# A fused attention and feed-forward kernel: the order of work inside an attention step is changed

## The reference

```
xn = layernorm(x);  Q = xn @ Wq / sqrt(32);  K = ctx @ Wk;  V = ctx @ Wv
scores = Q K^T + slope[head] * (key_pos - query_pos)     (masked)
w = softmax(scores);  x = x + tanh(g_xattn) * (w V) @ Wo
h = silu(bit_linear(layernorm(x), w_gate)) * bit_linear(layernorm(x), w_up)
x = x + tanh(g_ffn) * bit_linear(rms_norm(h), w_down)
```

## Time and profile before

| | |
|---|---|
| median of 3 runs | 536.34 us (533.21 to 541.49) |
| profiled execution: its own time | 538.78 us |
| its span, first to last instruction | 537.0 us |
| mean granted TensorE clock | 0.978 of full |
| TensorE busy | 478.4 us, 89% of the span |
| VectorE busy | 367.5 us, 68% |
| ScalarE busy | 329.6 us, 61% |
| GpSimd busy | 234.1 us, 44% |

### The profile page before, as it was taken

The page is one execution under the profiler, slowest core; times in us unless marked ns, Lnnn a source line. Parts: engine busy times, 40 slices in busy tenths (PEclk is TensorE's granted clock), DMA queues, the critical chain, the costliest instruction groups (busy, mean ns, idle before and its releaser), DMA issues.

```text
span 537.0 us, 8363 instructions
## 1 busy us (share of the span) xinstructions
PE 478.4 (89%) x2887; PEld 301.7 (56%) x2902; DVE 367.5 (68%) x674; ACT 329.6 (61%) x560; POOL 234.1 (44%) x250
## 2 busy tenths in 40 slices
PE   2599979998989999997889999879899999999966
PEld 1599979997954444443444445435454555555522
DVE  4777634466555888885697785376777777777782
ACT  0366637565436656664756676577677777777760
POOL 1000000000146687855263670157666667677641
PEclk9999998999899999998999999999999999999988
DMA  7869897999748788879667721002533333333323
GB/s 189 266 186 406 331 354 279 236 345 289 150 88 201 176 184 203 192 153 237 147 136 172 159 96 73 29 0 39 119 79 79 78 78 78 78 74 77 75 52 68
DMA packets 55875, 83.94 MB, mean 156 GB/s; under 512 B 30787, under 2 KB 42259, under 8 KB 53919
## 3 DMA queue, kind: packets, MB, share of 16 engines
q1 hardware_dynamic: 50654, 58.30, 43.2%
q0 software_dynamic: 3456, 12.58, 8.7%
q10 hardware_dynamic: 1728, 12.58, 6.8%
HBM read 57.94 MB, written 9.85 MB: 126 GB/s over the span
## 4 chain that ended last, share of the span: by engine, by line
PE 56%; DMA 14%; DVE 11%; ACT 9%; issue 5%; POOL 2%; SPq 1%; ACTq 0%; POOLq 0%; DVEq 0%
DMA ct<-ctx_t 7%; PE bank L1335 6%; PE wide L1410 6%; PE bank L1325 6%; PE wide L1311 6%; PE bank L1420 6%; PE wide L1242 6%; PE bank L1242 6%; PE bank L1338 5%; PE bank L1283 5%; DMA yq<-y_int 3%; ACT p_t L709 3%; DVE row_max L982 3%; DMA qs<-nm_t 2%; DMA wq_f<-wq 2%
## 5 line engine op out<-in xcount | busy, mean ns | idle before, releaser
L982 DVE TENSOR_REDUCE row_max<-wide 100x2 f32<-100x722 f32 x128 | 110.4, 903 | 37.0 <-PE wide L1311 36.9
L709 ACT ACTIVATE p_t<-bank 121x400 f32<-121x400 f32 x192 | 92.4, 504 | 53.0 <-PE bank L1325 49.1
L1410 PE MATMUL wide<-w_q,xq 128*128 128x512 bf16 x372 | 86.6, 384 | 2.2 <-ACT xq L758 1.2
L565 POOL TENSOR_TENSOR z<-h,lnw 128x512 f32<-128x512 f32 x48 | 61.5, 1282 | 32.8 <-DVE h L1099 25.1
L1410 PEld LDWEIGHTS wide<-w_q,xq 128*128 128x128 bf16 x384 | 36.7, 99 | 48.6 <-issue 5.6
L1311 PE MATMUL wide<-ks,qs 101*100 101x362 f32 x192 | 50.0, 348 | 10.0 <-DVE row_max L982 5.2
L519 POOL DMA_DIRECT2D quant_in<-w_ffn x24 | 14.3, 597 | 101.4 <-PE bank L1283 94.9
L1325 PE MATMUL bank<-qs,ks 103*121 103x400 f32 x144 | 50.9, 385 | 6.5 <-DMA qs<-nm_t 2.9
L805 ACT ACTIVATE act<-wide,small 128x512 f32<-128x512 f32 x50 | 33.9, 679 | 32.6 <-PE wide L1410 21.6
L1283 PE MATMUL bank<-wv_f,ct 128*121 128x128 f32 x384 | 47.5, 283 | 3.7 <-DMA ct<-ctx_t 3.7
L1420 PE MATMUL bank<-w_q,yq 128*128 128x512 bf16 x189 | 46.9, 392 | 3.3 <-DMA yq<-y_int 2.7
(11 more groups left out here) (159 smaller groups left out, 936.1 us busy)
## 6 DMA issues: line engine op xcount, KB each, us to landing
quant_in<-w_ffn POOLq DMA_DIRECT2D x24, 512.0 KB, 6.1
ct<-ctx_t SPq DMA_DIRECT2D x16, 722.0 KB, 10.2
ks<-k_all SPq DMA_DIRECT2D x36, 181.0 KB
q_scratch<-qhl SPq DMA_DIRECT2D x16, 400.0 KB, 7.7
abs_a<-w_ffn ACTq DMA_DIRECT2D x6, 1024.0 KB, 7.4
abs_b<-w_ffn ACTq DMA_DIRECT2D x6, 1024.0 KB, 8.9
qs<-q_scratch SPq DMA_DIRECT2D x12, 400.0 KB
xb<-x SPq DMA_DIRECT2D x12, 256.0 KB, 2.7
```

Of the source, the lines that this page charges most:

```text
L565: nc.gpsimd.tensor_tensor(z[par][0:rows, c], h[0:rows, c], lnw[0:rows, c], ALU.mult).then_inc(z_done, 1)
L709: nc.scalar.activation(p_t[:, j, :], bank[j % 2][0:KT, 0:HQ], ACT.Exp).then_inc(exp_done, 1)
L982: nc.vector.tensor_reduce(row_max[b % 2][:, 2 * u:2 * u + 2], wide[u % 2][0:SQ, :, 0:SK], AX_X, ALU.max).then_inc(s_maxed, 1)
L1410: mm = nc.tensor.matmul(wide[j % 2][0:rows, m, :], xq[:, c, 0:rows], w_q[:, m * C + c, 512 * j:512 * j + 512], start=(c == 0), stop=(c == ...
```

## The change

Three lists are changed. On TensorE the third values block of batch b-2 moves from slot 5, behind exponent blocks 1 and 2 of batch b-1, to slot 6, behind exponent block 3. On ScalarE exponential 3 of batch b-1 moves ahead of the eviction of batch b-2. On VectorE the first two normalising steps move from slot 3 to slot 0, and the third from slot 5 to slot 3. No instruction is added, removed or altered in size.

```diff
-NORMALISE_BEHIND = {3: (0, 1), 5: (2,)}
+NORMALISE_BEHIND = {0: (0, 1), 3: (2,)}
 BEHIND = {0: [("t", 2, 4), ("t", 2, 5), ("pv", 2, 0), ("turn", 1, 0), ("t", 2, 6), ("t", 2, 7)],
           1: [("t", 2, 8)],
           2: [("t", 2, 9), ("t", 2, 10)],
           3: [("t", 2, 11), ("pv", 2, 1)],
           4: [("t", 1, 0)],
-          5: [("t", 1, 1), ("t", 1, 2), ("pv", 2, 2)],
-          6: [("t", 1, 3)],
+          5: [("t", 1, 1), ("t", 1, 2)],
+          6: [("t", 1, 3), ("pv", 2, 2)],
           7: []}
...
                 if b >= 2:
                     exps(b - 2, 8, 9, 10, 11)
                 if b <= B:
-                    exps(b - 1, 0, 1, 2)
+                    exps(b - 1, 0, 1, 2, 3)
                 if 2 <= b <= B:
                     keep_pv(b - 2)
-                if b <= B:
-                    exps(b - 1, 3)
```

## The result

The changed kernel is slower: median 549.75 us of four executions (545.86 to 552.99) against 538.06 us (533.21 to 541.49). The ratio is 1.0239, 95% interval 1.0181 to 1.0297: clearly a loss, though whether it passes 2% is open. The forecast of 537.0 and its range to 542.0 were too low; none of the rivals named what happened.

A forecast was written before the change was run, and what follows sets the result against it. VectorE's score maxima were taken to hold TensorE in the attention steps. 8.7 - 2.6 - 1.0 - 0.5 - 1.9 - 3.8 = -1.1 us, slightly slower; median 537.4, given as 537.0, range 532 to 542.

The forecast's parts named there:

- Gain of 0.67 us a handover: Slot 0's scores on TensorE no longer wait for maxima 6: 0.67 us earlier, 13 times, 8.7 us gained.
- the 12.1 that the prediction named as a sign of being wrong: Attention steps averaging under 11.0 us or over 12.1 would show the prediction wrong.
- Eviction and exponential 3 cost nothing: On ScalarE, exponential 3 fills idle time and the moved eviction ends with slack of 0.15 and 0.23 us: no cost.
- Rival 4: Values block 0 waits 0.3 us each time for the eviction: 3.9 us, 541; chance 0.05.
- 0.2 us a step for maxima 1, 2.6 us: Slot-0 normalising on VectorE delays maxima 1, so scores 3 start at T + 4.9 instead of T + 4.70, 13 times.
- Collisions: GpSimd lengthens the second normalising step in slot 0, delaying scores 3 by 0.76 us in 5 of 13 steps: 3.8 us.
- Rival 2: GpSimd holds up the second slot-0 normalising step in 11 of 13 steps: 8.4 instead of 3.8 us, 542.0; chance 0.2.
- rival 3: GpSimd holds up the first normalising step too, 0.72 more in 5 colliding steps: 3.6 us, 541; chance 0.05.
- The one-off terms, 1.0 + 0.5 + 1.9 = 3.4 us: Batch 9's output-weight copy and batch 14's 0.64 us copy on ScalarE, and batch 10's weight residue on VectorE, delay single steps.
- Batch 10's residue ... 1.9 us: VectorE's 2.29 us weight residue queues before normalising and maxima 1: scores 3 near T + 6.9 instead of T + 4.98.
- The 0.5 us for the 0.64 us copy: ScalarE's copy behind batch 14 ends at T + 1.26, where exponential 4 wanted T + 0.77: 0.5 us.
- The batches' transfers keep their offsets: Transfers keep their place in the step; late maxima rows in single steps are taken as they are, no cost.

The follow-up runs named there:

- Kernel 1: The changed kernel with the normalising steps back in slots 3 and 5, TensorE's and ScalarE's new order kept: 536.13 us, ratio 1.0012.
- kernel 8: The changed kernel with output-weight copies in quarters over steps 10 to 13, their transfer in quarters over steps 5 to 8: 530.18 us, ratio 0.9849.
- kernel 13: Kernel 8 with VectorE's low part of the output weights whole again behind the maxima of batch 12: that step took 15.23 us, one execution.
- 2: The kernel before with only the normalising steps moved to slots 0 and 3: median 540.26 us, two executions left out (with them, 545.69).
- 3: The changed kernel with ScalarE's and VectorE's output-weight copies in quarters over steps 10 to 13: 540.60 us, ratio 1.0082.
- the two edits: On the changed kernel: output-weight copies in quarters (8.4 us saved) and the 1 MB output-weight transfer in quarters (10.4 us saved).
- kernel 16: Kernel 13 with batch 13's normalising alone back in slots 3 and 5: that step took 12.26 us, one execution.
- kernel 4: The changed kernel with the 1 MB output-weight transfer in quarters over steps 5 to 8: 539.36 us, ratio 1.0045.
- kernel 12: Kernel 8 with one normalising step each behind slots 3, 5 and 6, the low part's quarters moved: 525.38 us, ratio 0.9813.

## Why the prediction was wrong, point by point

- *Gain of 0.67 us a handover*: right. 0.41 us from scores 7 to slot 0, steps of 11.02 where nothing disturbs. That holds for 4 of the 13 steps; their average is 12.9 us, beyond the 12.1 that the prediction named as a sign of being wrong.
- *Eviction and exponential 3 cost nothing*: right. Kernel 1 has both and no loss; a wait of the values block on the eviction copy shows once in the attention waits, 0.2 us. Rival 4 is out.
- *0.2 us a step for maxima 1, 2.6 us*: too much. Scores 3 started at T + 4.69 in the step shown.
- *Collisions*: five predicted, five found in the 13 steps, and steps with one were 11.80 and 11.91 instead of 11.04, 0.8 us more. The count was right, in part by luck: the five other kernels with both steps in slot 0 throughout and the new order have 1 to 4. Rival 2, which had 11, was wrong; the instruction's median fell from 1.292 to 0.574 us. That the first step would be held up as well (rival 3, by the Trainium skill, SBUF — State Buffer, "Who interferes with whom") did not show: it took 0.56 to 0.58 us in all five. Single first steps of other kernels were held up, though: 1.42 us in kernel 8, 1.14 in 13. What was missed is that a collision in a step that already has a load adds to idle time behind which the clock fell, so that 0.76 us is not its whole price.
- *The one-off terms, 1.0 + 0.5 + 1.9 = 3.4 us*: this failed. "Batch 10's residue ... 1.9 us" was mis-sized. Against the same steps before, step 9 to 10 is 3.45 us longer and step 10 to 11 is 4.87; the terms said 0.35 and 1.2 net of the 0.65 that a step gains, or 1.1 and 2.0 with the collision that each had. The queue was drawn rightly, if 0.5 us too short beside the collision, but priced at full clock. What the runs showed in its place is idle time followed by a stretch at or near 1.2 GHz. That stretch costs 1.6 us in kernel 13's step. In step 10 to 11 of the changed kernel it is an estimated 2.8 us (5.8 us of full work at a granted clock of 0.51), on top of 3.2 us idle. The 0.5 us for the 0.64 us copy was too small as well: step 14 to 15 is 1.10 us longer than before, where 0.5, the collision and the gain make 0.6.
- *"The batches' transfers keep their offsets" and are not touched*: this failed too. The wait of step 8 to 9 grew from 2.87 to 5.4 us and the step by 2.66. Of the 2.5 us of waiting, about 0.7 is the offset, which did move: the maxima rows are issued sooner behind the 1 MB. Most of the rest is the 1 MB transfer itself, 13.1 us against 11.2. Why it took longer was not settled. Five profiles have it whole: 9.2, 10.0, 10.0, 11.2 and 13.1 us in kernels 1, 2, 3, before and changed, with waits of 0.3, 1.2, 2.2, 2.9 and 5.4 us, so part of it may be the luck of one execution. The medians speak for more than luck: quarters of the transfer save 10.4 us in the changed kernel, the larger of the two edits.
- *The last batch returns some tenths*: right, 13.95 against 14.63 us.

## What to carry to other kernels

A fixed order is tuned for its ordinary step, but it is the steps with something extra (a copy of weights, a big load) that decide whether a reordering pays: look through the order for one-off work before filling a gap, and spread that work first. Price idle time of TensorE together with the slow clock that may follow it, 1.6 us in two single steps here. And two dependent VectorE instructions in a row beside a busy GpSimd were dearer than the same two apart (1.29 against 0.57 us for the second).

## What the runs showed of the hardware

- Granted clock: 1.00 with one idle wait of 0.8 us in the step (kernel 16). After 1.52 and 1.70 us within 3 us it was 0.51 for 5.8 us of full work (changed kernel), and after 0.83 and 1.79 us it averaged 0.67 over 5.1 us (kernel 13). The longest single wait is not all: in the changed kernel's step 9 to 10 the two waits bracketed in the timeline before the fall are 0.77 and 0.76 us (at 263.14 and 265.67). Nor do the waits decide alone: after 0.67 and 0.91 us it stayed 1.00 (changed kernel, step 14 to 15), after 0.68 and 0.92 it averaged 0.67 over 5 us (kernel 4, the same step).
- VectorE beside GpSimd: the reductions from PSUM kept their duration in every step (0.911 us at most in the traces before and changed and in kernels 3, 8 and 12). The two-input first normalising step kept 0.56 to 0.58 us in most cases, with exceptions of up to 1.42 us (kernel 8). The second (scalar-tensor-tensor) went from 0.574 up to 1.47 us in the changed kernel, right behind the first; apart from it, at most 0.989 (kernel 12). The third, of the same kind and alone in its slot, took 0.57 us and once 1.02 in the changed kernel. Even a 100 x 16 one that takes 0.17 us took 1.04 beside a GpSimd instruction (276.05 above).
- A 6.2 KB transfer took 10.0 us from issue to release behind a 1 MB one from the same engine, with a 512 KB one of GpSimd's beside it. Over five traces the 1 MB took 9.2 to 13.1 us, and the release came 0.4 to 1.3 us after it had landed.
